# Encoder of a decoder block: attention outputs turned by VectorE block transposes, LayerNorm moved to ScalarE and GpSimd, and the carried attention state held in full 128x128 block-diagonal tiles

## The reference, cut to what matters

```
q = elu(x @ Wq + bq) + 1;  k = elu(x @ Wk + bk) + 1;  v = x @ Wv + bv      # 16 heads of 16
A = (q k^T) * tril within chunks of 128 tokens
KV, z = sums of k v^T and of k over the earlier chunks of the sequence      # carried state
out = (A v + q KV) / (rowsum(A) + q z + 1e-6)
x = layer_norm(x + out @ Wo + bo, g1, be1)
x = layer_norm(x + gelu(x @ W1 + b1) @ W2 + b2, g2, be2)                    # 256 -> 1024 -> 256
```

## Time and profile before

| what | value |
|---|---|
| median of the timed runs | 1613.78 us |
| profiled execution: span from first to last instruction | 1609.4 us |
| what lies around the span, against the median | 4.4 us |
| TensorE matmul busy | 1523.1 us (95%) |
| VectorE busy | 1287.7 us (80%) |
| ScalarE busy | 951.3 us (59%) |
| GpSimd busy | 802.8 us (50%) |
| chain that ended last: TensorE, VectorE | 83%, 11% |
| granted TensorE clock, mean | 0.986 |

### The profile page before, as it was taken

The page is one execution under the profiler, slowest core; times in us unless marked ns, Lnnn a source line. Parts: engine busy times, 40 slices in busy tenths (PEclk is TensorE's granted clock), DMA queues, the critical chain, the costliest instruction groups (busy, mean ns, idle before and its releaser), DMA issues.

```text
span 1609.4 us, 38530 instructions
## 1 busy us (share of the span) xinstructions
PE 1523.1 (95%) x15894; PEld 1225.0 (76%) x15894; DVE 1287.7 (80%) x2566; ACT 951.3 (59%) x1516; POOL 802.8 (50%) x580
## 2 busy tenths in 40 slices
PE   3799999999999999999999999999998999999998
PEld 3688888888888888888888888888886566666434
DVE  3777888888888888888878878888776788988556
ACT  3465556665556665565655556655534777777445
POOL 3354445545455454554555535654455366664424
PEclk8899999999999999999999999999999999999999
DMA  6110011201121001210012100112024444443001
GB/s 137 37 62 15 21 24 41 66 9 21 25 67 46 5 19 24 67 47 11 12 24 67 47 19 11 18 41 50 1 49 121 138 136 139 143 139 95 1 0 53
DMA packets 98351, 82.52 MB, mean 51 GB/s; under 512 B 23040, under 2 KB 86400, under 8 KB 98176
## 3 DMA queue, kind: packets, MB, share of 16 engines
q1 hardware_dynamic: 98176, 80.06, 18.5%
HBM read 50.78 MB, written 14.68 MB: 41 GB/s over the span
## 4 chain that ended last, share of the span: by engine, by line
PE 83%; DVE 11%; issue 2%; ACT 1%; SPq 1%; POOL 1%; DMA 0%; ACTq 0%; DVEq 0%
PE e_pr L170 10%; PE e_pr L172 8%; PE e_pr L171 8%; PE e_tr L428 6%; PE e_sc L401 6%; PE x_psO L1366 4%; PE e_tr L170 4%; PE e_tr L172 3%; PE e_tr L171 3%; PE e_sc L170 3%; PE e_sc L172 3%; PE e_sc L171 3%; PE e_tr L438 3%; PE x_psT L1351 2%; PE f_bank L1912 2%
## 5 line engine op out<-in xcount | busy, mean ns | idle before, releaser
L715 POOL TENSOR_TENSOR e_h_lo<-e_h_f,e_h_hi 128x512 fp32r<-128x512 f32 x192 | 265.7, 1388 | 279.1 <-ACT e_h_hi L557 275.2
L805 DVE TENSOR_TENSOR e_am<-e_sc,c_amask 128x1024 f32<-128x1024 f32 x192 | 225.7, 1216 | 18.3 <-PE e_sc L401 18.3
L556 ACT ACTIVATE e_h_f<-e_pr,e_h_bias 128x512 f32<-128x512 f32 x192 | 132.1, 688 | 174.3 <-PE e_pr L172 170.6
L1676 DVE TENSOR_REDUCE x_mx<-x_psS 128x4 f32<-128x1024 f32 x128 | 150.9, 1219 | 25.8 <-PE x_psS L1329 24.9
L170 PE MATMUL e_tr<-e_W_hi,e_h_hi 128*128 128x256 f32 x576 | 163.2, 283 | 8.1 <-DVE X L762 8.1
L170 PE MATMUL e_pr<-e_yT_hi,e_W_hi 128*128 128x512 f32 x384 | 168.6, 439 | 0.0
L171 PE MATMUL e_tr<-e_W_lo,e_h_hi 128*128 128x256 f32 x576 | 160.8, 279 | 0.0
L172 PE MATMUL e_tr<-e_W_hi,e_h_lo 128*128 128x256 f32 x576 | 160.7, 279 | 0.0
L172 PE MATMUL e_pr<-e_yT_hi,e_W_lo 128*128 128x512 f32 x384 | 152.3, 397 | 0.0
L171 PE MATMUL e_pr<-e_yT_lo,e_W_hi 128*128 128x512 f32 x384 | 151.8, 395 | 0.0
L1502 ACT ACTIVATE x_ex<-x_psT 128x1024 f32<-128x1024 f32 x128 | 130.9, 1022 | 26.5 <-PE x_psT L1351 21.6
(11 more groups left out here) (284 smaller groups left out, 4320.5 us busy)
## 6 DMA issues: line engine op xcount, KB each, us to landing
e_raw_m<-in_L_attn_W_dram SPq DMA_DIRECT2D x12, 1024.0 KB, 5.3
x_qs<-query_rows SPq DMA_DIRECT2D x48, 256.0 KB
e_x_raw<-e_a_tok SPq DMA_DIRECT2D x368, 32.0 KB, 1.9
x_ks<-key_rows SPq DMA_DIRECT2D x48, 128.0 KB, 2.8
query_rows<-x_q_hi SPq DMA_DIRECT2D x16, 256.0 KB, 2.1
query_rows<-x_q_lo SPq DMA_DIRECT2D x16, 256.0 KB, 2.3
x_ctok<-in_ctx_dram SPq DMA_DIRECT2D x8, 256.0 KB, 3.3
x_xo<-in_x_dram SPq DMA_DIRECT2D x8, 256.0 KB, 3.8
```

What stands on the lines that cost most here:

```text
L556: act.activation(h_f[:, m % HR, :], ps_pr[m % 2][:, :], ACT.Gelu, bias=h_bias[:, m:m + 1])
L715: pool.tensor_tensor(h_lo[:, m, :], h_f[:, m % HR, :], h_hi[:, m, :].bitcast(F32), ALU.subtract).then_inc(h_lo_done, 1)
L805: dve.tensor_tensor(am[:, s % 2, c, :, :, :], ps_sc[:, :, c * 2 * P:(c + 1) * 2 * P].rearrange("p r (h n) -> p r h n", n=P), amask[:, :].u ...
L1676: dve.tensor_reduce(mx[:, N % 2, :, 0:HG].rearrange("p i (a h) -> p h a i", a=2)[:, pair], ps_s[pair][:, :, :].rearrange("p a (i j) -> p a ...
```

## The change

**Attention output.** The matmuls of `attend` write their output into PSUM in an order such that 32x32 block transposes of VectorE turn it: `to_tokens(s)` becomes one VectorE transpose of 128x512 from PSUM into `ob` for each block. Denominators, reciprocals, division are done for two blocks at a time (`pair`), and a second VectorE transpose (`to_features`) gives `aT`, again for two blocks. ScalarE makes its high part (`attn_hi(pair)`), VectorE its low part (`attn_lo(pair)`). `out_copy` and both groups of TensorE transposes (L438, L467) are gone. TensorE's product with `Wo` is in two halves, with `qk(0)` and `qk(1)` of the next tile between them.

**Carried state.** Four matmuls of full height, 128 x 136 outputs, replace the sixteen; four VectorE instructions mask them with `headmask` into `kv`, now block-diagonal; and four full 128x128 matmuls (`carried(s)`, called ahead of the loop for `s = 0`, and after `mlp_up(3)` for `s = 2`) replace the eight small ones.

**LayerNorm.** VectorE keeps the sums and makes the negative mean; GpSimd makes the power and `shift = -mean * rs`; ScalarE applies both (`normed`, 4 activations of 128x256); GpSimd multiplies by the gain (`gained`, 128x1024). The bias of the first LayerNorm is folded into the part that goes to TensorE (`be1_columns`) and into the row added later; that of the second is a further GpSimd addition (`shifted`, 128x1024).

**Order.** The transposition of the next input (`x_transpose`) stands after `residual(2, 2)`; `x_lo` is split around the division; the conversion of `W1` is in the first step of its layer, after `ktok`, not at the end of the last step of the layer before; `W2` is converted in two halves, the weights of the attention after `ktok`; the addition of `bo` stands ahead of the hidden units on GpSimd. Two small loads (`be1_columns`) are added at the start.

The diff, cut to its core:

```
 TensorE
-                            for r in range(NR):
-                                mm = pe.matmul(ps_sc[rows, KV_BANK[b], c * 2 * HX:(c + 1) * 2 * HX], ktok[:, b, c, rows],
-                                               vx[:, 2 * b + 1, c * HC + 2 * r:c * HC + 2 * r + 2, 0:HX], ...)
+                            mm = pe.matmul(ps_sc[:, KV_BANK[b], c * HC * HX:(c + 1) * HC * HX], ktok[:, b, c, :],
+                                           vx[:, 2 * b + 1, c * HC:(c + 1) * HC, 0:HX], start=True, stop=True)
+                def carried(s):
+                    if s > 1:
+                        pe.wait_ge(ob_done, SB * t + s - 1)
+                    elif mlp:
+                        pe.wait_ge(yT_lo_done, 2 * u + 2)
+                    pe.wait_ge(kv_done, 4 * t + 2 * (s // 2) + 2)
+                    for g in range(4):
+                        pe.matmul(out_block(s, g, slice(0, P)), kv[:, s // 2, g // 2, g % 2, :, :], qkT[:, g // 2, blk(s)],
+                                  start=(g == 0), stop=False, skip_group_check=True)
...
-                    if attn:
-                        to_tokens(s)
+                    if attn and s == 1:
+                        carried(2)
...
-                            mm = pe.transpose(ps_tr[c][:, blk(s)], a_tok[:, s, blk(c)], ident[:, :])
...
                     for s in range(SB):
+                        if following and mlp and s == 2:
+                            pe.wait_ge(gelu_done, FC * u + FC - 1)
+                            qk(0)
+                            pe.wait_ge(gelu_done, FC * u + FC)
+                            qk(1)
+                        pe.wait_ge(aT_lo_done, 2 * t + s // 2 + 1)
 ScalarE
+                def normed(i, n, tile):
+                    act.wait_ge(rs_done[i], LNS[i] * n + 2)
+                    for s in range(SB):
+                        x = X[:, tile * SB + s, :]
+                        act.activation(x, x, ACT.Identity, bias=shift[i][:, s:s + 1], scale=rs[i][:, s:s + 1]).then_inc(xn_done[i], 1)
...
                         exp(j)
+                        if mlp and j == 1:
+                            normed(1, u, q)
...
                 for s in range(SB):
-                    if attn:
-                        out_copy(s)
                     if mlp:
                         gelu(2 + s)
+                    if s == 1 and u > 0:
+                        normed(2, u - 1, (q - 1) % NT)
                     if following and s in (1, 2):
                         x_hi(t + 1, s - 1)
+                    if s == 2 and attn:
+                        attn_hi(0)
...
                 if mlp:
                     gelu(6)
+                    gelu(7)
                 if attn:
+                    attn_hi(1)
 GpSimd
                 if mlp:
-                    rsqrt(1, ve_done[1], u + 1)
+                    rsqrt(1, u)
+                    if u > 1:
+                        gained(2, u - 2, (q - 2) % NT)
+                    gained(1, u, q)
+                    if u > 1:
+                        shifted(u - 2, (q - 2) % NT)
...
+                if q < 0 or (q == 0 and l > 0):
+                    w_m("W1", w1_hi, l, w1_lo, 0)
+                    w_m("W1", w1_hi, l, w1_lo, 1)
...
+                    if following:
+                        add_row((q + 2) % NT, rows_a["bo"], xT_tr, t + 3, bo_loaded, 16 * (l2 + 1), xbo_done)
 VectorE
+                dve.tensor_scalar(ve[i][:, :].unsqueeze(2), mv[i][:, :, 1:2], LN_EPS, None, ALU.add).then_inc(ve_done[i], 1)
+                dve.tensor_scalar(nm[i][:, :].unsqueeze(2), mv[i][:, :, 0:1], -1.0, None, ALU.mult).then_inc(ve_done[i], 1)
...
+                def to_tokens(s):
+                    dve.wait_ge(out_full, SB * t + s + 1)
+                    dve.transpose(ob[:, s % 2, :, :].rearrange("p g n -> p (g n)"), ps_tr[s % 2][:, :]).then_inc(ob_done, 1)
...
-                for s in range(SB):
-                    if attn and s + 1 < SB:
-                        mask(s + 1)
-                    if prev and s == 0:
-                        centre(2, d, last, rows_m["g2"], ln2_rows_loaded, rows)
-                    if prev and s == 2 and u < final:
-                        scale(2, d, last, rows_m["be2"], range(0, 2))
-                    if attn:
-                        divide(s)
+                if attn:
+                    mask(1)
+                    to_tokens(0)
+                    mask(2)
+                    to_tokens(1)
+                    denominators(0)
+                    mask(3)
+                    reciprocals(0)
+                if following:
+                    x_lo(t + 1, 0)
+                if attn:
+                    divide(0)
+                    to_tokens(2)
+                    to_features(0)
+                if following:
+                    x_lo(t + 1, 1)
+                if attn:
+                    to_tokens(3)
+                    attn_lo(0)
+                    denominators(1)
+                    reciprocals(1)
+                    divide(1)
+                    to_features(1)
...
                 if attn:
+                    attn_lo(1)
```

More of the change, by code:

```diff
@@ L445, in step @@
                     mlp_up(1)
+                if attn:
+                    carried(0)
                 if u == final:
@@ L663, in w_o, with w_m @@
                 lo_part("Wo", raw_a[:, 3].rearrange("p c n -> p (c n)"), 1, o_lo)
-            def w_m(w, ready, value, done):
-                pool.wait_ge(ready, value)
-                lo_part(w, raw_m, 4, done)
+            def w_m(w, ready, layer, done, part):
+                flat_hi = hi[w][:, :, :].rearrange("p c n -> p (c n)").bitcast(F32)
+                flat_lo = lo[w][:, :, :].rearrange("p c n -> p (c n)")
+                pool.wait_ge(ready, 2 * layer + part + 1)
+                for j in (2 * part, 2 * part + 1):
+                    cols = slice(j * TT, (j + 1) * TT)
+                    a = pool.tensor_tensor(flat_lo[:, cols], raw_m[:, cols], flat_hi[:, cols], ALU.subtract)
+                if part == 1:
+                    a.then_inc(done, 1)
             w_qkv(1)
@@ L821, in phi, with attn_lo @@
+                def attn_lo(pair):
+                    cols = slice(2 * P * pair, 2 * P * (pair + 1))
+                    dve.wait_ge(aT_hi_done, 2 * t + pair + 1)
+                    low(aT_lo[:, :, cols], aT[:, :, cols], aT_hi[:, :, cols]).then_inc(aT_lo_done, 1)
                 def phi(j):
@@ L898, in step @@
                     residual(2, 2, d, last, m_full, xb2_done)
-                    for s in range(SB - 1):
-                        spread(2, s, d, last)
+                if following:
+                    x_transpose(t + 1, (q + 2) % NT)
                 if attn:
@@ L930, in step @@
                     cross.queries_lo(0, 0, cross.early(2))
-                    scale(2, d, last, rows_m["be2"])
                 if u == final - 1:
+                    dve.wait_ge(ln_done[2], final - 2)
                     cross.encoder_stats(0)
-                if following:
-                    x_lo(t + 1)
                 if attn:
-                    for c in range(KC):
-                        dve.wait_ge(aT_hi_done, 2 * t + c + 1)
-                        low(aT_lo[:, c, :], ps_tr[c][:, :], aT_hi[:, c, :]).then_inc(aT_lo_done, 1)
+                    attn_lo(1)
                 if u == final - 1:
```

369 lines of the change are left out of this document (188 added, 181 removed).

## The result

The changed kernel takes 1686.8 us (median of 4 runs, 1683.91 to 1689.07) against 1613.18 for the kernel before on the same chip: a ratio of 1.0458, 95% interval [1.0443, 1.0473]. It is slower by 74 us, where 19 less were forecast. Its profiled span is 1687.3 us.

The account below looks back on a forecast made before the run. TensorE's list was taken to bound each step. 18 steps at 0.6 us and 5 at 1.6 us saved 18.8 us: span 1609.4 to 1590.6, plus 4.4 around it, 1595 us; range 1560 to 1622.

Parts of the forecast that it names:

- The new stall: End of the loop: TensorE's mlp_up(7) waits 1.1 us for gelu(5), which stands behind attn_hi(0) on ScalarE.
- plain step: Encoder step other than a layer's first: 46.7 us of TensorE plus 1.1 us of waiting, 47.8 us, 0.6 less than now.
- Rivals 1 and 2: End of loop: 1, no new stall, 1565 us (0.20); 2, x_lo and division slow, stall 2.1 us, 1615 us (0.17).
- Rival 3: VectorE's small instructions after mask(0) held by GpSimd at SBUF, mask(1) about 1 us late: 1637 us, chance 0.13.
- LayerNorm: First LayerNorm's new path over GpSimd and ScalarE is hidden by 3 us; later x_transpose leaves its transfers some 15 us.
- GpSimd has room: GpSimd's three more instructions of 2.4 us in a step fit: about 35 of 47 us busy.
- Once a layer: A layer's first step, with W1's conversion moved there and centre off VectorE: 48.8 us, 1.6 less than 50.36.
- Start and hand-over: Two added loads at the start and the hand-over to cross attention: nothing, within 3 us each way.
- The test named in the prediction: TensorE waiting at the transposition of X or mlp_up(0) would mean the moved LayerNorm or W1 was not covered.

Follow-up runs that it names:

- w1_short: Changed kernel; bv, bo and W2 loads ahead of the x transfers, W1's low part cut to 32 of each 512 columns from the second layer: 1624.05 us.
- bo_first: Changed kernel; in a layer's third step SyncE loads the next layer's bv and bo ahead of the 16 x transfers: 1640.55 us, 1.0172.
- bo_late_add: Changed kernel; loads stay late, but in the third step GpSimd adds bo behind the hidden units: 1641.4 us, 1.0173.
- bo_early_before: Kernel before; in a layer's third step GpSimd adds bo ahead of the hidden units: 1640.72 us, 1.0188.
- w2_first: Changed kernel; in a layer's first step only the W2 load is moved ahead of the x transfers: 1679.58 us, 1.041.
- mask_short: Changed kernel; bv, bo, W2 loads ahead of transfers, mask(2) ahead of to_tokens(0), state by small matmuls, W1's low part cut from layer two: 1618.23 us.
- small_only: Changed kernel; bv, bo and W2 loads ahead of the x transfers, state built by the sixteen small matmuls: 1630.91 us, 1.0122.
- mask_first: Changed kernel; bv, bo and W2 loads ahead of the x transfers, mask(2) ahead of to_tokens(0) on VectorE: 1631.39 us, 1.0117.
- mask_small: Changed kernel; bv, bo and W2 loads ahead of transfers, mask(2) ahead of to_tokens(0), state built by sixteen small matmuls: 1631.83 us, 1.0119.
- w1_back: Changed kernel; W1 converted and W2 loaded in the layer before, bv/bo loads ahead of transfers, x_transpose earlier, attn_hi(0) behind gelu(5), state by small matmuls: 1688.03 us, 1.0475.

## Why the prediction was wrong

**The durations were right, but one.** Four full matmuls of `carried` took 0.98 us from start to start (1.00 forecast from the earlier trace rows), the state 0.93 (1.06), block transposes of 512 columns 0.70 to 0.72 (0.70), four `normed` 2.08 (2.3), and `x_lo` and the first division 0.62 to 0.69 (0.69). The second division took 1.50, beside GpSimd's low parts of the hidden units.

By the 81 ns of the Trainium skill (TensorE: Matmul & The Clock Gate, Back-to-back issue gap) eight records would take 0.65 us; they took 0.98, so the row of the same shape was the better guide.

**The new stall was right.** In a plain step of the changed kernel:

```profile
364.44 0.50 PE L175 MATMUL e_pr<-e_yT_hi,e_W_hi 128*128 128x512 f32 x1 [1.05 <-ACT e_h_hi L557]
```

1.05 us for a forecast of 1.1, and plain steps of 47.66 and 47.90 for 47.8. Rivals 1 and 2 fall with it. Rival 3, the port, had the wrong place. Its mechanism is in this plain step: the epsilon took 1.08 us at 346.98 beside GpSimd, where it took 0.17 at 373.16. But `mask(1)` then still waited 0.51 us for `scores(1)`, so it did not hold up the mask. It cost at the low part of the queries next to `W1`'s conversion, once in a layer, for up to 10 us by w1_short.

**The step that failed.** It is this one, under "LayerNorm": "`x_transpose` later on VectorE leaves its 16 transfers some 15 us, before `x_hi`". I asked only who needs the transfers' data. Nothing was said of what is queued behind them on SyncE: `bv`, `bo` and `W2`. And the addition of `bo` ahead of the hidden units, which is named in the change, got no term at all; "GpSimd has room" counted its busy time and not its waits. In its place the runs showed GpSimd waiting 14.65 us for `bo`, and ScalarE and then TensorE (6.59 us) behind it: a third step of 58.55 us for 47.8. bo_first and bo_late_add remove 46 of the 74 us, each alone.

How much of the 46 comes from the later transfers, and how much from `normed(2)` on ScalarE, which now waits for GpSimd ahead of `gelu(4)`, was not measured. bo_early_before doesn't tell, since its 29 us came by way of `centre`.

Against the forecast the span is 96.7 us too long (77.9 more in place of 18.8 less): 53.5 in the third steps, 35.3 in the first ones (five forecast at 1.6 us less, the sixth at 0.6), 7.5 at the ends and 0.4 in the plain ones. So the plain step, on which the prediction spent most of its working, is nearly exact, and most of the error lies in what it passed over.

**"Once a layer" failed too.** 48.8 us were forecast for a first step, 54.78 came. I took the low parts of `W1` as a question of when they end, and not of whom they hold up meanwhile (w1_short: 10 us), and the late `W2` (w2_first: 7 us) and the shared buffer were left out. With both loads moved, the mask ahead and `W1`'s low part cut, mask_short's first steps are still 51.24 us, 2.4 above the forecast; the cause of that rest was not found.

**The ends.** Start and hand-over were put at 0 within 3 us each way: +1.7 and +5.8. TensorE's wait at the transposition of `X` in the last step, before and after:

```profile
1199.05 1.27 PE L361 MATMUL e_tr<-c_ident,X 128*128 128x128 f32 x8 [2.67 <-DVE X L762]
```

```profile
1274.29 1.11 PE L363 MATMUL e_tr<-c_ident,X 128*128 128x128 f32 x4 [6.09 <-DVE X L798]
```

It waits for a residual on VectorE (1273.82). That stands behind statistics of the cross attention, which wait 6.84 us for GpSimd, and GpSimd is busy with `gained` twice and `shifted`, the LayerNorm work that the change gave it:

```profile
1262.16 4.80 POOL L756 TENSOR_TENSOR X<-X,e_g 128x1024 f32<-128x1024 f32 x2
1266.93 2.36 POOL L762 TENSOR_TENSOR X<-X,e_be 128x1024 f32<-128x1024 f32 x1
...
1270.59 1.26 POOL L1644 TENSOR_TENSOR x_xw<-x_xw,x_xo 128x512 f32<-128x512 f32 x1
...
1271.88 0.75 DVE L1716 BATCH_NORM_STATS2 x_st<-x_xw 128x6 f32<-128x256 f32 x2 [6.84 <-POOL x_xw L1644]
```

It is the same fault once more: GpSimd's added work was counted as busy time, and not by who waits behind it. No run changed this, so its share of the 5.8 us, 3.4 by the two waits of TensorE, is read from the traces only.

**The test named in the prediction** ("wrong at its root if TensorE waits at the transposition of `X` or at `mlp_up(0)`") saw only the smaller part. TensorE does wait at the transposition of `X` in a first step (1.77 us), for VectorE's residual beside `W1`'s conversion. The large wait came at `mlp_up(6)`, behind SyncE, GpSimd and ScalarE in turn.

**What stays open.** No variant beats the kernel before. The best that computes everything is small_only, with mask_first and mask_small level within their intervals. Its span is 23.7 us longer: +19.3 in the first steps (53.55 us), +0.7 in the third, +7.1 behind them and +0.5 ahead, with -3.9 from the plain ones. Whether another place for `W1`'s low part would make the change pay is open: the one place tried (w1_back) was worse, in a kernel with other edits.

## What to carry to other kernels

Where a change moves a group of transfers on a queue, list every load behind it, and for each the first instruction that waits for it and what stands behind that on its engine. An engine that is 59% busy and in order can hold up the whole kernel with one early wait; count when its inputs come, not its free time. Where two or three chains end within a microsecond of each other, to remove one wait shows the next: sum the margins before you move anything.

## What the runs showed of the hardware

After a wait of 6.59 us TensorE's clock was at 1.2 GHz for about 8 us, and 512-column matmuls came 0.43 us apart in place of 0.23. I had not counted it. It adds some 3 us to the long wait worked out above, and 1.5 us in some of mask_short's first steps, whose single waits are under 3 us. The view by stretch, in the third step and behind it:

```profile
410.00:417.00 7.00, 0.43 (x2) 0.00 (x0) 1.14 (x2) 3.77 (x8) 5.56 (x6) 0.83 0.00 0
417.00:425.00 8.00, 7.43 (x21) 5.75 (x22) 5.88 (x10) 4.97 (x9) 4.44 (x4) 0.51 0.00 1
425.00:432.00 7.00, 7.00 (x40) 6.03 (x39) 5.69 (x17) 4.38 (x7) 1.60 (x2) 1.00 0.00 0
```

SyncE's queue took 0.65 to 0.72 us for each transfer of 32 KB, so 16 of them closed it for 10.35 to 11.5 us, although one landed 1.9 us after its issue (median).

VectorE instructions beside GpSimd grew by more than their own length. Four `centre` of 128x256 took 1.66 us in the kernel before and 6.15 in bo_early_before, where GpSimd worked without a gap. A small one grew most in proportion: the addition of the epsilon to the denominators (128x32) took 0.18 us in the changed kernel's third step, and 1.27 us in small_only beside GpSimd's low parts of hidden units.
